# Order and grain in four places of a transformer kernel on one core

## The reference, cut to what matters

```python
x = L0(x, ctx, ctx)          # two cross attentions (16 heads of 128, one learnt key) and an MLP 512-2048-512
def L1(x, ctx):              # the second block: one head of width 512
    q, k, v = x @ w_q.T, ctx @ w_k.T, ctx @ w_v.T
    probs = softmax(q @ k.T / sqrt(512))
    return x + alpha * ((probs @ v) @ w_o.T)
x = L2(ctx, x, mask)         # latents = x, keys from ctx and x, 16 heads, rmsnorm, MLP, residual
def L3(x, ctx, mask):        # the fourth block: 16 heads of 32, then an MLP
    q = layer_norm(x) @ q_w + q_b;  k, v = ctx @ k_w + k_b, ctx @ v_w + v_b
    x = x + softmax(mask(q @ k.T / sqrt(32))) @ v @ cproj_w + cproj_b
    return x + gelu(layer_norm(x) @ fc_w + fc_b) @ proj_w + proj_b
```

## Time and profile before

| | |
|---|---|
| median of 3 runs | 2831.62 us (2829.5 to 2832.07) |
| profiled execution, its own time | 2831.26 us |
| its span, first to last instruction | 2829.2 us |
| TensorE busy | 2663.9 us, 94% |
| VectorE busy | 1462.0 us, 52% |
| ScalarE busy | 782.2 us, 28% |
| GpSimd busy | 381.7 us, 13% |
| mean granted TensorE clock | 0.972 of full speed |
| DMA | 118.28 MB, mean 42 GB/s |

### The profile page before, as it was taken

One profiled execution on the slowest core, in us unless ns is written; L12 is line 12 of the kernel. 1 busy time (PEld: TensorE's weight loads), 2 busy tenths in 40 slices (PEclk: granted clock), 3 DMA queues, 4 the chain that ended last, 5 costly groups with the idle time before them and its releaser, 6 DMA issues. The chain is left out here.

```text
span 2829.2 us, 30362 instructions
## 1 busy us (share of the span) xinstructions
PE 2663.9 (94%) x12328; PEld 1942.8 (69%) x12328; DVE 1462.0 (52%) x2282; ACT 782.2 (28%) x1363; POOL 381.7 (13%) x246
## 2 busy tenths in 40 slices
PE   9999999999799999889999999879999889799999
PEld 7778777877678887645444444358888656578887
DVE  6465566555753443335445454375344586763442
ACT  4322243223221111115344343431111243321110
POOL 0000000000120000015243343331000310120000
PEclk9999999999999999899999999889999999999999
DMA  4101110110100001211112121020000100100001
GB/s 188 60 30 42 49 60 30 45 45 1 63 16 16 30 1 55 87 48 48 48 48 63 39 62 49 24 108 30 16 15 1 68 1 0 64 1 30 30 1 60
DMA packets 35556, 118.28 MB, mean 42 GB/s; under 512 B 8021, under 2 KB 8150, under 8 KB 25946
## 3 DMA queue, kind: packets, MB, share of 16 engines
q1 hardware_dynamic: 35418, 116.35, 12.4%
HBM read 81.18 MB, written 7.34 MB: 31 GB/s over the span
## 5 line engine op out<-in xcount | busy, mean ns | idle before, releaser
L1541 DVE TENSOR_REDUCE l_top<-l_slot 128x1 f32<-128x512 f32 x256 | 170.4, 679 | 192.2 <-PE l_slot L1352 191.5
L1491 ACT ACTIVATE l_weighed<-l_across 128x512 f32<-128x512 f32 (+1 forms) x320 | 183.0, 594 | 300.2 <-PE l_across L1374 296.6
L389 PE MATMUL l_wide<-l_key_map,l_norm 128*128 128x260 f32 x1024 | 235.3, 383 | 2.7 <-ACT l_norm L544 2.3
L389 PEld LDWEIGHTS l_wide<-l_key_map,l_norm 128*128 128x128 f32 x1024 | 191.8, 190 | 32.1 <-ACT l_norm L544 2.7
L1222 POOL TENSOR_TENSOR l_paired<-l_weighed 128x2048 f32<-128x2048 f32 x32 | 145.5, 4546 | 396.7 <-ACT l_weighed L1491 336.4
L1374 PE MATMUL l_across<-l_q_stack,l_k_stack 99*128 99x512 f32 (+1 forms) x320 | 186.8, 588 | 12.1 <-ACT l_weighed L1491 9.1
L725 DVE TENSOR_TENSOR x<-l_added,x 128x512 f32<-128x512 f32 x128 | 87.1, 687 | 82.0 <-PE l_added L131 60.5
L1374 PEld LDWEIGHTS l_across<-l_q_stack,l_k_stack 99*128 99x128 f32 (+1 forms) x320 | 59.2, 186 | 97.6 <-issue 61.6
L1352 PE MATMUL l_slot<-l_k_stack,l_q_stack 97*128 97x512 f32 x256 | 112.2, 439 | 14.3 <-DMA l_k_stack<-l_k_parts 6.4
L2319 ACT ACTIVATE l3m_hidden<-l3m_up,columns 128x512 f32<-128x512 f32 x64 | 44.1, 690 | 272.8 <-PE l3m_up L131 262.0
L2319 ACT ACTIVATE l0m_hidden<-l0m_up,columns 128x512 f32<-128x512 f32 x64 | 44.2, 692 | 271.0 <-PE l0m_up L131 258.5
(11 more groups left out here) (379 smaller groups left out, 5971.4 us busy)
## 6 DMA issues: line engine op xcount, KB each, us to landing
l_k_stack<-l_k_parts SPq DMA_DIRECT2D x192, 72.0 KB, 2.0
l_q_stack<-l_q_parts SPq DMA_DIRECT2D x192, 64.0 KB, 2.0
l_wk<-in_weights SPq DMA_DIRECT2D x9, 1024.0 KB, 4.7
l_wv<-in_weights SPq DMA_DIRECT2D x9, 1024.0 KB, 4.8
l_wo<-in_weights SPq DMA_DIRECT2D x9, 1024.0 KB, 4.8
l_wqT<-in_weights SPq DMA_DIRECT2D x8, 1024.0 KB, 6.9
l0m_raw<-in_weights SPq DMA_DIRECT2D x8, 1024.0 KB, 4.7
l2m_raw<-in_weights SPq DMA_DIRECT2D x8, 1024.0 KB, 4.8
```

What stands on the lines that cost most here:

```text
L389: last = pe.matmul(wide[:, j, 0:W], norm[:, k, at:at + P], key_map[:, k, b, :, :].rearrange("p h c -> p (h c)"), start=k == 0, stop=k == K ...
L1491: act.activation(weighed[0:height(c), (CHUNKS * g + c) % RING, j, :], across[0:height(c), use % 2, :], ACT.Exp)\
L1541: dve.tensor_reduce(top[:, t, j:j + 1], slot[:, i % 2, :], AX.X, ALU.max, negate=True).then_inc(s["top_ready"], 1)
```

## The change

Four places are touched. No arithmetic changes.

1. Second block's attention. TensorE makes the scores of batch 0 before the first value map, turns x of batches 2 and 3 together, puts the output tiles of batch 0 among the scores of batch 2 and the second value map behind them. VectorE and ScalarE follow; add_outs can now take single tiles.
2. Fourth block's VectorE order. take_values(0) and take_values(1) each come one shift earlier, and for batches 1 and 2 the add of output tile 2 comes before shift(b, 3).
3. First MLP weights. GpSimd's cast and subtraction of w1 and w2 for f = 0 go over 512 columns each, four times, and TensorE waits for each quarter of w1. The counts become KT + f (splits).
4. The last batch is stored tile by tile.

```diff
@@ l1_attention, TensorE
             project("key_map", wq, "wq_loaded", keys)
-            map_values(0)
             for j in range(TPB):
                 logits(0, j)
+            map_values(0)
             for j in range(TPB):
                 logits(1, j)
             turn_x(2)
+            turn_x(3)
+            turn_probs(0)
+            logits(2, 0)
+            logits(2, 1)
+            out(0, 0)
+            logits(2, 2)
+            out(0, 1)
+            logits(2, 3)
+            out(0, 2)
+            turn_probs(1)
+            out(0, 3)
             map_values(1)
-            turn_x(3)
-            for b in range(2):
-                turn_probs(b)
-                logits(b + 2, 0)
-                for t in range(TPB):
-                    if t + 1 < TPB:
-                        logits(b + 2, t + 1)
-                    out(b, t)
+            for t in range(TPB):
+                logits(3, t)
+                out(1, t)
             turn_probs(2)
@@ ScalarE
+            exps(0)
             high_map(0)
-            exps(0)
             exps(1)
             take_x(2)
-            high_map(1)
             take_x(3)
             high_probs(0)
             exps(2)
             high_probs(1)
+            high_map(1)
             exps(3)
@@ VectorE
+            rows_max(0)
             low_map(0)
-            rows_max(0)
+            normalise(0)
             rows_max(1)
-            normalise(0)
             take_x(2)
-            normalise(1)
-            low_map(1)
             take_x(3)
             low_probs(0)
-            add_outs(0)
+            normalise(1)
+            add_outs(0, (0, 1))
             rows_max(2)
+            low_probs(1)
+            add_outs(0, (2, 3))
             normalise(2)
-            low_probs(1)
-            add_outs(1)
+            low_map(1)
+            add_outs(1, (0, 1, 2))
             rows_max(3)
+            low_probs(2)
+            add_outs(1, (3,))
             normalise(3)
-            low_probs(2)
             add_outs(2)
@@ l3_attention, VectorE
                 else:
                     lows(b + 1, 0)
                     lows(b + 1, 1)
+                    take_values(0)
                 shift(b, 1)
...
                     lows(b + 1, 2)
                     lows(b + 1, 3)
+                    take_values(1)
...
-                else:
-                    take_values(0)
                 normalise(b, 1)
                 if not more:
                     add_out(b - 1, 1)
-                if b == 0:
-                    take_values(1)
+                elif b:
+                    add_out(b - 1, 2)
                 shift(b, 3)
-                if b:
+                if not more:
                     add_out(b - 1, 2)
-                if not more:
                     add_out(b - 1, 3)
@@ mlp_stage
+        def splits(f):
+
+            return KT + f
...
-                for c in range(B):
+                for c in range(B - 1):
...
+                for t in range(TILES - TPB, TILES):
+                    sp.wait_ge(down_added, (FB - 1) * DOWNS + t + 1)
+                    sp.dma_start(out_dram[:, t, :], n.x[:, t, :]).then_inc(stored, 16)
...
-            pool.tensor_copy(w1h[:, :, :], raw1[:, :, :]).then_inc(w1_high, 1)
-            pool.wait_ge(w1_high, 1)
-            pool.tensor_tensor(w1l[:, :, :], raw1[:, :, :], w1h[:, :, :].bitcast(F32), ALU.subtract).then_inc(w1_ready, 1)
+            for k in range(KT):
+                pool.tensor_copy(w1h[:, k, :], raw1[:, k, :]).then_inc(w1_high, 1)
+                pool.wait_ge(w1_high, k + 1)
+                pool.tensor_tensor(w1l[:, k, :], raw1[:, k, :], w1h[:, k, :].bitcast(F32), ALU.subtract).then_inc(w1_ready, 1)
...
                         if m == 0 and f == 0:
+                            if c == 0:
+                                pe.wait_ge(w1_ready, k + 1)
                             pe.wait_ge(low_ready, c * KT + k + 1)
...
-                    pe.wait_ge(w2_ready, f + 1)
+                    pe.wait_ge(w2_ready, splits(f))
```

More of the change, by code:

```diff
@@ L1052, in normalise, with add_outs @@
                                   inverse[:, u, :].unsqueeze(2).unsqueeze(3).to_broadcast([P, TPB, 2, C]), ALU.mult).then_inc(s["probs_ready"], 1)
-            def add_outs(b):
-                for j in range(TPB):
+            def add_outs(b, tiles=range(TPB)):
+                for j in tiles:
                     t = b * TPB + j
@@ L2208, in _ @@
             for f in range(1, FB):
-                sp.wait_ge(w1_ready, f)
+                sp.wait_ge(w1_ready, splits(f - 1))
                 sp.dma_start(raw1[:, :, :], n.block(first, f)).then_inc(raw1_loaded, 16)
-                sp.wait_ge(w2_ready, f)
+                sp.wait_ge(w2_ready, splits(f - 1))
                 sp.dma_start(raw2[:, :, :], n.block(second, f)).then_inc(raw2_loaded, 16)
             if out_dram is not None:
-                for c in range(B):
+                for c in range(B - 1):
                     sp.wait_ge(down_added, (FB - 1) * DOWNS + (c + 1) * TPB)
                     sp.dma_start(out_dram[:, c * TPB:(c + 1) * TPB, :], n.x[:, c * TPB:(c + 1) * TPB, :]).then_inc(stored, 16)
-                sp.wait_ge(stored, 16 * B)
+                for t in range(TILES - TPB, TILES):
+                    sp.wait_ge(down_added, (FB - 1) * DOWNS + t + 1)
+                    sp.dma_start(out_dram[:, t, :], n.x[:, t, :]).then_inc(stored, 16)
+                sp.wait_ge(stored, 16 * (B - 1 + TPB))
         @block.gpsimd
@@ L2221, in _ @@
             pool.wait_ge(raw1_loaded, 16)
-            pool.tensor_copy(w1h[:, :, :], raw1[:, :, :]).then_inc(w1_high, 1)
-            pool.wait_ge(w1_high, 1)
-            pool.tensor_tensor(w1l[:, :, :], raw1[:, :, :], w1h[:, :, :].bitcast(F32), ALU.subtract).then_inc(w1_ready, 1)
+            for k in range(KT):
+                pool.tensor_copy(w1h[:, k, :], raw1[:, k, :]).then_inc(w1_high, 1)
+                pool.wait_ge(w1_high, k + 1)
+                pool.tensor_tensor(w1l[:, k, :], raw1[:, k, :], w1h[:, k, :].bitcast(F32), ALU.subtract).then_inc(w1_ready, 1)
             pool.wait_ge(raw2_loaded, 16)
-            pool.tensor_copy(w2h[:, :, :], raw2[:, :, :]).then_inc(w2_high, 1)
-            pool.wait_ge(w2_high, 1)
-            pool.tensor_tensor(w2l[:, :, :], raw2[:, :, :], w2h[:, :, :].bitcast(F32), ALU.subtract).then_inc(w2_ready, 1)
+            for k in range(KT):
+                pool.tensor_copy(w2h[:, k, :], raw2[:, k, :]).then_inc(w2_high, 1)
+                pool.wait_ge(w2_high, k + 1)
+                pool.tensor_tensor(w2l[:, k, :], raw2[:, k, :], w2h[:, k, :].bitcast(F32), ALU.subtract).then_inc(w2_ready, 1)
             pool.wait_ge(bias_loaded, 16)
@@ L2247, in ups @@
                 for m in blocks:
-                    if m == 0 and c == 0:
-                        pe.wait_ge(w1_ready, f + 1)
+                    if m == 0 and c == 0 and f:
+                        pe.wait_ge(w1_ready, splits(f))
                     if f or c:
@@ L2389, in split_w1 @@
                 dve.tensor_copy(w1h[:, :, :], raw1[:, :, :]).then_inc(w1_high, 1)
-                dve.wait_ge(w1_high, f + 1)
+                dve.wait_ge(w1_high, splits(f))
                 dve.tensor_tensor(w1l[:, :, :], raw1[:, :, :], w1h[:, :, :].bitcast(F32), ALU.subtract).then_inc(w1_ready, 1)
@@ L2395, in split_w2 @@
                 dve.tensor_copy(w2h[:, :, :], raw2[:, :, :]).then_inc(w2_high, 1)
-                dve.wait_ge(w2_high, f + 1)
+                dve.wait_ge(w2_high, splits(f))
                 dve.tensor_tensor(w2l[:, :, :], raw2[:, :, :], w2h[:, :, :].bitcast(F32), ALU.subtract).then_inc(w2_ready, 1)
```

## The result

The changed kernel takes 2801.95 us in the median of 4 runs (2800.08 to 2804.11), the kernel before 2830.98 (4 runs); the ratio is 0.9899, 95% interval 0.9886 to 0.9912. The profiled execution took 2802.86, its span is 2800.8, 28.4 shorter than before. Busy time on TensorE fell by 13.3 us (2663.9 to 2650.6), the granted clock rose from 0.972 to 0.980. A shorter busy time for the same 12328 matmuls, beside a higher granted clock, I read as time that is no longer spent at half clock.

What follows compares the result with a forecast made beforehand. The prediction took TensorE's queue (busy 94%) to bound the kernel. Gains of 6.4 + 1.4 + 2.4 + 7.75 + 1.9 = 19.85 us off 2831.26, with 0.36 added, gave 2811.8, range 2804 to 2823.

Steps and rivals of the forecast that it cites:

- Part 3: First MLP weights in quarters: shorter holds between GpSimd and VectorE gain 7.75 us over l0m, l2m and l3m.
- the w2 term: In l2m, quarters of w2 let the hidden split through sooner, shortening TensorE's 4.87 us wait: 5.1 us gained.
- the start: At l2m's start, a tiny chain of three meets three quarters instead of one hold: 0.3 us gained.
- l3m: Fourth block's MLP: small TENSOR_SCALAR through earlier, then four scalings alternating with quarters; second turn earlier, 2.35 us gained.
- l0m: First block's MLP: rows(1) 0.75 us earlier, but one more quarter met; 0 gained, ends -1.3 and 1.5.
- Part 1: Second block's attention reordered: ends at 1191.5, 6.4 us gained; next block's loads stay hidden by 2 to 4 us.
- Part 2: Fourth block's VectorE order: 1.4 us from batch 0's 5.31 wait, 1.2 each from batches 1 and 2.
- Part 4: Last batch stored by tile: the final 256 KB store lands in 2.4 to 2.5 us, 1.9 us gained.
- One turn per pair: Rival, MLPs: VectorE gets in only between GpSimd's cast and subtraction; MLPs gain 2, total 2817.5 us; chance 0.16.
- Starvation: Rival, MLPs: a stream of 16 GpSimd quarters shuts VectorE out; total 2837 us; chance 0.05.
- The attention orders trade waits: Rival, second and fourth blocks: VectorE sets the second block's pace; both reorderings bring 3, total 2819 us; chance 0.07.
- The clock holds: Rival, second and fourth blocks: the clock stays up behind the remaining waits; 25.6 gained, total 2806 us; chance 0.12.

Runs made afterwards that it cites:

- after_again: The changed kernel with no edit, profiled a second time and timed in more rounds: 2802.83 us, ratio 0.9901 to the kernel before.
- w2_whole: The changed kernel with w2 cast and subtracted whole again, w1 still in quarters: 2817.24 us, ratio 0.9952 to the kernel before.
- before: First profile of the kernel before the change, the one the prediction read: 2831.26 us; median of its 4 runs 2830.98.
- after: First profile of the changed kernel, all four parts in: 2802.86 us; median of its 4 runs 2801.95, ratio 0.9899.

## Why the prediction was wrong

The direction, the places and nearly every mechanism were right; the sum was 8 to 9 short of what the runs gave (28.0 and 29.0). Over all profiles of the table, the stages with the old code against those with the change (five against five in the MLPs, six to eight elsewhere) give 5.6 for the second block, 4.5 for the fourth, 1.9, 8.1 and 3.9 for l0m, l2m and l3m, 2.3 for the store: 26.3, within the interval of 28.0 (23.2 to 32.5) of after_again and that of the first 29.0 (24.9 to 32.3). So 6.5 of the shortfall stand in the stages, nearly all in part 3; the other 2 to 3 no run assigns, and they are inside the noise.

- **Part 3 is the step that failed: 7.75 forecast, 13.9 measured.** Three terms in it. *l2m*, 5.4 against 8.1: the w2 term was 5.1 and is 5.8 (w2_whole); the start was "0.3", which holds only against the execution I read: when GpSimd's CAST comes 0.04 to 0.16 us sooner behind the first scaling, the kernel before loses another 3.3, in three of five profiles with this code. That is 2.0 in the mean, which the forecast put at nothing. *l3m*, 2.35 against 3.9: the small TENSOR_SCALAR was not held by a quarter at all (0.17, I had it through at 9.6 us into the stage, it was at 8.5), and the second scaling took 3.70 where I had 4.7, so the turn came 3.25 earlier. With the clock held in both, l3m gave 3.5 (374.4 to 370.9); the rest of the 3.9 is the clock. *l0m*, 0 against 1.9: I overlooked that its first scaling, 3.5 with the whole CAST, would be 2.2, and counted one more wait for the second.
- **Part 1: 6.4 forecast, 5.6 in the mean and 7.3 in the profile.** Its end was put at 1191.5; it came at 1190.7 (1188.87 plus the 1.78 by which the stage began earlier), since the clock was back sooner than I had it. The loads stayed hidden, but the margin was misread. I had counted to the end of their traffic, 13.5 behind low_map(1); the landing, for which the stage waits, came 14.8 behind it in before (1180.04) and 16.0 in after (1188.71, the last add at 1188.87). In the other seven profiles with this part 1.4 to 2.8 us were spare. The sentence that each of the three waits of before contains a whole softmax is wrong for the third (1.41): there only ScalarE's high half and VectorE's low half lie between the turn and the output.
- **Part 2: 3.8 forecast, 4.5 in the mean.** Batch 0 gave 1.8 (forecast 1.4), batch 1 1.1 (1.2), batch 2 2.7 in after with the clock held and 1.1 in after_again without it. "Worth 1.4 of 5.31" was right: the turn began at once when VectorE's last normalisation ended (2284.69). The third query waited 2.30, where 2.5 was said.
- **Part 4: 1.9 forecast, 2.3 measured**, in each of eight profiles: a 256 KB store lands in 2.1 rather than 2.4.
- **The rivals.** "One turn per pair" did not come: one instruction of VectorE gets in at every change, between cast and subtraction and between subtraction and cast. Starvation did not come in the quarters. It stays real beside the 16 additions of the bias row: there a CAST of VectorE that takes 0.42 free took 8.29 in before, 9.18 in l3m of after, and at most 1.6 in after_again. "The attention orders trade waits" (3 for parts 1 and 2 together) did not come either, with 5.6 and 4.5. "The clock holds" was right at one place, the fourth block's batch 2, in some executions.
- **The range** was worked out as if one profile stood for the kernel before. Its executions differ by 13 us. The second value of l2m lies on the slow side only and is gone with the change; the clock falls or holds in both kernels. A forecast of the mean has to price both.

What stays open: which of the two clock values comes in an execution, why VectorE gets in between a subtraction and the next cast but, in most profiles, not between the additions, and the 2 to 3 us between 26.3 by stages and the 28 to 29 measured.

## What to carry to other kernels

When two engines shut each other out, price the length of the one's instructions against the number of the other's, since here one got in at each change between cast and subtraction (but not between the additions of the bias row). From the same start four scalings took 7.93 with w2 whole, 7.32 in halves and 3.70 in quarters: cutting by four paid well, cutting by two hardly. Look for places in the trace where a start a few tenths of a us earlier or later would pass or miss such a hold, and count the gain over both outcomes. And before a difference of a few us is explained, profile the same program twice, stage by stage.

## What the runs showed of the hardware that I had not expected

- In l2m a CAST of GpSimd that starts 0.81 us behind VectorE's first of four scalings makes the four last 7.62, one that starts 0.85 behind 3.31: 4.3 us from 0.04.
- Statistics are not held. In the kernel before, four of them in l0m last 2.46 right beside a subtraction of GpSimd (VectorE, then GpSimd), as long as ahead of it (2.47):

```profile
751.72 2.46 DVE L2357 BATCH_NORM_STATS2 l0m_stats<-x 128x6 f32<-128x512 f32 x4
```

```profile
751.60 4.59 POOL L2224 TENSOR_TENSOR l0m_w1l<-l0m_raw,l0m_w1h 128x2048 fp32r<-128x2048 f32 x1
```

- One program's executions lie within 13 us, and its granted clock between 0.971 and 0.977; the falls come behind idles of 0.6 to 2.4 us, or do not, with the same idles.
